# A fused attention and expert block: maxima 30 ahead of the scores, Q loads ahead of the shift, heads turned a step later

## The chip, the cores and the metric

The kernel runs on one core of a Trainium2 chip (eight cores; one is used). The metric is the device time of one execution in microseconds (us). Three executions of the kernel before took 608.63, 608.9 and 609.54 us; their median is 608.9.

## The reference

`x` has shape 8 x 512 x 128 (batch, token, channel). A modulation of 6 x 128 numbers per batch is computed from `c`. The block is attention and then a mixture of experts, each on a normalized and modulated input and each added back through a gate:

```python
mod = (_silu(L0_c) @ L0_wmod).reshape(L0_c.shape[0], 6, 1, -1)
h = _layernorm(x, axis=-1) * (1 + ca) + sa
x = x + ga * _L0_attn_ref(h, L0_attn_Wq, L0_attn_Wk, L0_attn_Wv)
h = _layernorm(x, axis=-1) * (1 + cb) + sb
x = x + gb * _L0_ffn_ref(h, ...)
# attention: 16 heads of 8 for the queries, one shared key and value head of 8
dist = jnp.einsum('bhqd,bkd->bhqk', q, k) * scale
dist = jax.nn.softmax(dist, axis=-1)
att = jnp.einsum('bhqk,bkd->bhqd', dist, v)
# experts: 8, of which the best 2 of each token, hidden size 512, gelu, weights by softmax of the two logits
```

## The kernel before, in words

The attention works on 8 batches of 16 heads. A group is 4 heads (`G`) of one batch, so there are 32 groups (`GROUPS`), four to a batch (`NG`). Each group has four steps `s` (128 keys each in the scores), and in each step a counter `j` runs from 0 to 3. Three products are made for a group:

- **maxima** (`maximum`, line 1052): 16 units of four matmuls each write a 128 x 512 block of scores into one of three banks of a ring; VectorE reduces it to a negative maximum per query (line 1364, `neg_max`).
- **scores** (`scores`, line 1068): K times Q, with the maximum already subtracted. For that the negative maxima must be in three extra rows of Q. The way there: VectorE transposes the group's maxima (`turn_maxima`, line 1372), GpSimd splits them into three bf16 parts (`split`, lines 76 to 79), and SyncE copies these with three DMAs into Q (`shift`, line 948). ScalarE takes the exponential (line 1252).
- **values** (`values`, line 1079): the exponentials times V, summed over the steps in one bank. ScalarE copies the bank out (line 1244), and SyncE spreads it over two tensors with five DMAs (`regroup`, lines 958 and 959).

Each engine has its own list of instructions in the order in which the code writes them, and waits by semaphores. DMAs are issued from SyncE's list in that order too. In the loop over `g`, `s` and `j` TensorE makes one unit of the maxima of group `g + 2` for each `j`, so the maxima run 32 units ahead of the scores; before the loop the first 32 units are made with little else beside them. VectorE's reductions follow in the same order. The scores of step 0 wait for the group's `shift_loaded`.

Q, K and V have two buffers, one batch in each. A **refill** loads the batch after next in six of the loop's groups (4, 8, ..., 24): SyncE waits until all values of the group before are done and issues ten DMAs, Q and K in turn, then V (`load_operands`, lines 148, 152 and 156). Their rows of Q are 24 partitions of 16 KB, and three such loads fill it.

When a batch's four groups are done, its sums and its heads are turned by TensorE (`turn_sums`, line 1089; `turn_heads`, line 1097) through the same ring of three banks, and copied out by ScalarE (`sums_out`, `heads_out`). This falls into the groups 5, 9, 13, ..., 29. From group 9 on these also hold the rank matmuls of an earlier batch (lines 1134 and 1135). `ring_order` lists all users of the ring in order; who frees a bank follows from it. A unit waits for the taking of the unit three places earlier.

GpSimd does the routing of earlier batches beside the splits (with indirect DMAs, line 812). The seventh batch is routed by VectorE in group 30. After the loop, 71 tiles of 128 tokens run through the experts (lines 1142, 1151 and 1162).

Of the kernel before, what the change touches and what calls it, by code (L numbers as in the profile page):

```python
# [13 lines left out]
B, S, D = 8, 512, 128  # L14
NH, DK = 16, 8
# [66 lines left out]
def adaln_block(nc, x, wq_t, wkv_t, router_t, w1_t, b1_t, w2_t, b2, c_t, wmod, constants, shift_rows, fill_rows, out):  # L82
# [8 lines left out]
    with ctx:  # L91
# [52 lines left out]
        def load_operands(eng, b, p, loaded, begin=0, end=3):  # L144

            for blk in range(begin, end):
# [3 lines left out]
                              ).then_inc(loaded[p], 16)  # L150
                for n in (0, 1):
# [3 lines left out]
            if begin == 0:  # L155
                eng.dma_start(V[p][:].rearrange("p t c -> p (t c)"), v_cols[b]).then_inc(loaded[p], 16)
# [472 lines left out]

        def ring_order():  # L630

            units = [("maximum", n // (G * T), n // G % T, n % G) for n in range(2 * G * T)]
            for g in range(GROUPS):
                for s in range(T):
                    for j in range(G):
                        if g + 2 < GROUPS:
                            units.append(("maximum", g + 2, s, j))
# [302 lines left out]
        with nc.Block() as block:  # L940
            @block.sync
            def _(eng):
# [65 lines left out]
                load_operands(eng, 1, 1, batch_loaded, 0, 3)  # L1008
# [34 lines left out]
            def _(eng):  # L1043
# [125 lines left out]
                for g in (0, 1):  # L1169
                    for n in range(G * T):  # L1170
                        b = g * (G * T) + n - 5
                        if b >= 0 and b % 3 == 0 and b // 3 < B:
                            modulation_row(b // 3)
                        maximum(g, n // G, n % G)
                eng.wait_ge(row_out, START + B)
                eng.wait_ge(rows_loaded, START + 7 * 16)
                for g in range(GROUPS):
                    for s in range(T):
                        for j in range(G):
                            if g + 2 < GROUPS:  # L1180
                                maximum(g + 2, s, j)
# [4 lines left out]
                            if s == 1 and j == 3 and batch_at(g, 1) is not None:  # L1186
# [52 lines left out]
            def _(eng):  # L1239
# [120 lines left out]
            def _(eng):  # L1360
# [119 lines left out]

                prepare_vector(eng)
# [5 lines left out]
                for n in range(2 * G * T):  # L1487
                    take_maximum(n // (G * T), n // G % T, n % G)
# [221 lines left out]
```

## Time and profile before

| what | us |
|---|---|
| median of three executions | 608.9 |
| the profiled execution's own time | 614.37 |
| its span, first to last instruction | 612.6 |
| TensorE matmul busy | 544.6 (89%) |
| VectorE busy | 503.6 (82%) |
| ScalarE busy | 435.9 (71%) |
| GpSimd busy | 306.5 (50%) |

The attention loop goes from about 66 to 422 us, the experts from there to the end. Rows of a timeline merge neighbours: "x16" is 16 instructions, the first number is the start of the first and the second the time from there to the end of the last. The bracket at the end is the engine's idle time before and who ended it.

### The profile page before, as it was taken

What the parts mean: (1) busy time and instruction counts of PE and PEld (TensorE: products, weight loads), DVE (VectorE), ACT (ScalarE), POOL (GpSimd) and SP (SyncE); (2) the same over time, 40 slices, a digit from 0 to 9 for tenths busy, and PEclk for the clock granted to TensorE, in tenths of its full rate; (3) what the DMA queues carried; (4) which work ended last, traced back from release to release, by engine and by line L of the source; (5) the groups of instructions that cost most, each with busy time, mean ns of one, the idle gap of its engine ahead of it and who ended that gap; (6) DMA issues with size and microseconds to landing.
All of it is one profiled execution on the core that took longest, in us unless ns stands there. A gap on an engine that the chain in (4) does not pass through costs nothing.

```text
span 612.6 us, 21006 instructions
## 1 busy us (share of the span) xinstructions
PE 544.6 (89%) x7675; PEld 337.3 (55%) x7675; DVE 503.6 (82%) x1190; ACT 435.9 (71%) x724; POOL 306.5 (50%) x581
## 2 busy tenths in 40 slices
PE   2669999999999999999999999968886896999970
PEld 2222345555555545545545545425876885999960
DVE  5878999999999899899899899876564673755697
ACT  5674588889888889889888888768443432566661
POOL 2615010134475676675775766760555465455470
PEclk9888999999999999999999999989997998899995
DMA  6289500220310410401401401111322122232645
GB/s 191 64 275 353 137 8 13 52 59 10 76 42 23 103 33 24 115 23 28 112 23 27 116 18 28 28 41 42 84 71 65 57 73 74 76 86 60 202 139 176
DMA packets 54484, 49.44 MB, mean 81 GB/s; under 512 B 20224, under 2 KB 48944, under 8 KB 53664
## 3 DMA queue, kind: packets, MB, share of 16 engines
q1 hardware_dynamic: 46864, 36.89, 22.4%
q0 software_dynamic: 4320, 9.38, 4.7%
q10 hardware_dynamic: 3200, 1.84, 1.0%
q8 instruction: 63, 1.03, 0.7%
q14 instruction: 37, 0.30, 0.2%
HBM read 29.40 MB, written 17.10 MB: 76 GB/s over the span
## 4 chain that ended last, share of the span: by engine, by line
PE 55%; DVE 15%; POOL 6%; issue 6%; another core or an unknown queue 5%; DMA 4%; SPq 3%; ACT 3%; DVEq 1%; POOLq 0%; ACTq 0%
PE ps L1052 13%; PE ps L1068 12%; PE ps L1079 12%; DVE neg_max L1364 7%; PE ps L1162 7%; PE ps L1151 7%; DMA Q<-max_parts 3%; POOL h_sorted L812 2%; ACT parts L1291 1%; PE ps L1142 1%; PE ps L1109 1%; DVE P L286 1%; SPq L948 1%; PE ps L1116 1%
## 5 line engine op out<-in xcount | busy, mean ns | idle before, releaser
L1364 DVE TENSOR_REDUCE neg_max<-ps 128x1 f32<-128x512 f32 x512 | 322.3, 681 | 19.3 <-PE ps L1052 15.9
L1252 ACT ACTIVATE P<-ps,zero 128x1024 f32<-128x1024 f32 x256 | 280.1, 1117 | 52.5 <-PE ps L1068 45.4
L1052 PE MATMUL ps<-K,Q 128*32 128x512 bf16 x2048 | 196.4, 382 | 4.3 <-DVE neg_max L1364 3.6
L1068 PE MATMUL ps<-Q,K 128*32 128x512 bf16 x2048 | 156.5, 381 | 5.7 <-ACT P L1252 3.6
L1079 PE MATMUL ps<-P,V 128*32 128x256 f32 x2048 | 157.8, 382 | 0.5 <-ACT P L1252 0.4
L1602 POOL DMA_INDIRECT y_rows<-P,to_now x71 | 72.2, 1017 | 87.5 <-DVE P L1427 46.0
L1291 ACT ACTIVATE parts<-ps,parts 128x128 f32<-128x128 f32 x228 | 63.8, 381 | 61.0 <-remote 23.7
L1052 PEld LDWEIGHTS ps<-K,Q 128*32 128x32 bf16 x2048 | 55.0, 96 | 74.7 <-DVE neg_max L1364 28.8
L1079 PEld LDWEIGHTS ps<-P,V 128*32 128x32 f32 x2048 | 61.9, 110 | 48.7 <-issue 3.0
L1068 PEld LDWEIGHTS ps<-Q,K 128*32 128x32 bf16 x2048 | 53.9, 97 | 61.1 <-ACT P L1252 11.6
L812 POOL DMA_INDIRECT h_sorted<-diag,slot x64 | 65.8, 1028 | 33.7 <-POOL max_parts L79 16.5
L1151 PE MATMUL ps<-parts 128*128 128x128 f32 x456 | 65.0, 284 | 7.4 <-issue 7.0
L1162 PE MATMUL ps<-W,parts 128*128 x456 | 63.0, 282 | 1.9 <-ACT parts L1291 0.9
L1151 PEld LDWEIGHTS ps<-parts 128*128 128x128 f32 x456 | 57.7, 196 | 10.6 <-issue 9.2
L1162 PEld LDWEIGHTS ps<-W,parts 128*128 128x128 f32 x456 | 57.2, 197 | 3.1 <-issue 2.7
L1408 DVE COPY parts<-W 128x644 f32 x57 | 30.4, 532 | 18.5 <-issue 10.7
L76 POOL CAST max_parts<-neg_max_T 128x32 bf16<-128x32 f32 x32 | 6.8, 213 | 72.6 <-DVE neg_max_T L1372 71.2
L1427 DVE TENSOR_TENSOR P<-ps,parts 128x128 f32<-128x128 f32 x57 | 16.2, 283 | 26.5 <-remote 16.3
L1291 ACT ACTIVATE P<-ps,P 128x128 f32<-128x128 f32 x56 | 16.0, 374 | 17.3 <-remote 8.2
L1142 PE MATMUL ps<-consts,xs 128*128 128x128 f32 x71 | 20.1, 283 | 1.2 <-DMA xs<-h_sorted 1.1
L1415 DVE COPY parts<-ps 128x128 f32<-128x128 f32 x57 | 16.2, 284 | 4.4 <-PE ps L1142 3.0
L1244 ACT COPY att_u<-ps 128x512 f32<-128x512 f32 x32 | 18.5, 579 | 0.8 <-PE ps L1079 0.8
(241 smaller groups left out, 542.9 us busy)
## 6 DMA issues: line engine op xcount, KB each, us to landing
Q<-q_parts SPq DMA_DIRECT2D x24, 384.0 KB
xs<-h_sorted SPq DMA_DIRECT2D x71, 72.0 KB
W<-w_t SPq DMA_DIRECT2D x2, 2048.0 KB, 11.0
q_parts<-parts SPq DMA_DIRECT2D x8, 384.0 KB, 3.7
Q<-y_rows SPq DMA_DIRECT2D x6, 512.0 KB
diag<-att_u SPq DMA_DIRECT2D x128, 16.0 KB
Q<-max_parts SPq DMA_DIRECT2D x96, 4.0 KB
out<-Q SPq DMA_DIRECT2D x6, 256.0 KB, 2.8
```

Of the source, the lines that this page charges most:

```text
L812: eng.indirect_dma_start(h_sorted, bass.IndirectOffsetOnAxis(ap=slot[p][:, k, t:t + 1], axis=0), hs[p][:, t, :], None).then_inc(routed[p], 16)
L1052: ins = eng.matmul(ring_bank(*unit)[QUAD * q:QUAD * (q + 1), :], Q[buffer_of(g)][:, g % NG * G + q, at:at + QUAD], K[buffer_of(g)][:, 0, : ...
L1068: ins = eng.matmul(to, K[p][:, 1, at:at + QUAD], Q[p][:, first:first + 2, some], start=True, stop=True, tile_position=(0, QUAD * q))
L1079: ins = eng.matmul(bank(7)[QUAD * j:QUAD * (j + 1), some], V[buffer_of(g)][:, s, :], P[s % 2][:, j, some], start=(s == 0 and u == 0), stop ...
L1142: eng.transpose(bank(TURN_BANK[t % 2])[:, 0:TS], xs[t % XD][:, 0:D], ident).then_inc(xsT_done, 1)
L1151: ins = eng.matmul(bank(t % UD)[:, TS * c:TS * (c + 1)], w1_now[t % HD][:, 128 * c:128 * (c + 1)], xsT[t % HD], start=True, stop=True)
L1162: ins = eng.matmul(bank(DOWN_BANK[t % 2])[:, 0:D], hid[t % HD][:, c, :], W2[:, bass.ds(e, 1), c, :].rearrange("p a d -> p (a d)"), start=( ...
L1252: nc.scalar.activation(P[s % 2][:, :, HALF * u:HALF * (u + 1)], bank(2 * u, 2).rearrange("p (j t) -> p j t", j=G), ACT.Exp, bias=zero[:], ...
L1291: nc.scalar.activation(hid[t % HD][:, c, :], bank(t % UD)[:, TS * c:TS * (c + 1)], ACT.Gelu, bias=w1_now[t % HD][:, F + c:F + c + 1]).then ...
L1364: eng.tensor_reduce(neg_max[g % 2][:, at:at + 1], ring_bank("maximum", g, s, j), AX.X, ALU.max, negate=True).then_inc(ring_used, 1)
L1408: eng.tensor_copy(w1_now[t % HD], W1[:, bass.ds(e, 1), :].rearrange("p a d -> p (a d)")).then_inc(w_copied, 1)
L1602: eng.indirect_dma_start(y_rows, bass.IndirectOffsetOnAxis(ap=to_now[t % YD], axis=0), ys[t % YD], None).then_inc(scattered[t % YD], 16)
```

## The change

It has three parts.

1. `LEAD` is 30 (2 x 16 - 2): 30 units of maxima are made ahead of the loop, and in the loop the unit of 30 places on. The transpose of a group's maxima comes at `j == 2` of step 0 where it came at `j == 0`. The routing of the seventh batch on VectorE moves from the head of group 30 behind its third unit.
2. `turn_heads` moves from `s == 1, j == 3` to `s == 2, j == 1`, and ScalarE's copy of it from the first to the second exponential of step 2.
3. The loads are split in two. `load_queries` (three DMAs) stands ahead of the shift in a refill group and waits for the scores of the group before; `load_others` (six of K, one of V) stays behind the regroup and waits for the values of the group before. The loads of the first two batches now also issue Q first and then K.

```diff
-        def load_operands(eng, b, p, loaded, begin=0, end=3):
+        def load_operands(eng, b, p, loaded):
+            load_queries(eng, b, p, loaded)
+            load_others(eng, b, p, loaded)
...
+        LEAD = 2 * G * T - 2
+        def place_of(n):
+            return n // (G * T), n // G % T, n % G
+        def ahead_of_scores(g, s, j):
+            return place_of((g * T + s) * G + j + LEAD)
...
                 for g in range(GROUPS):
                     b = g // NG + 1
+                    refill = g % NG == 0 and 2 <= b < B
+                    if refill:
+                        eng.wait_ge(score_done, START + g * T * 2)
+                        load_queries(eng, b, b % 2, batch_loaded)
                     if g + 1 < GROUPS:
                         shift(g + 1)
                     if 0 < g < GROUPS - 1:
                         regroup(g - 1)
-                    if g % NG == 0 and 2 <= b < B:
+                    if refill:
                         eng.wait_ge(pv_done, START + g * T * 2)
-                        load_operands(eng, b, b % 2, batch_loaded)
+                        load_others(eng, b, b % 2, batch_loaded)
...
-                            if g + 2 < GROUPS:
-                                maximum(g + 2, s, j)
+                            if ahead_of_scores(g, s, j)[0] < GROUPS:
+                                maximum(*ahead_of_scores(g, s, j))
...
-                            if s == 1 and j == 3 and batch_at(g, 1) is not None:
+                            if s == 2 and j == 1 and batch_at(g, 1) is not None:
                                 turn_heads(batch_at(g, 1))
...
-                            if s == 2 and u == 0 and batch_at(g, 1) is not None:
+                            if s == 2 and u == 1 and batch_at(g, 1) is not None:
                                 heads_out(batch_at(g, 1))
...
-                            if s == 0 and j == 0 and g + 2 < GROUPS:
+                            if s == 0 and j == 2 and g + 2 < GROUPS:
                                 turn_maxima(g + 1)
+                            if (g, s, j) == (GROUPS - 2, 0, 2):
+                                turn_maxima(g + 1)
+                                seventh_routed()
```

On SyncE, the DMAs of the first refill group. `Q<-max_parts` is the shift, `diag<-att_u` and `sums_T<-att_u` are the regroup, the others load the batch. Before, the rows are these:

```order
L948 DMA Q1<-max_parts1 1x64x32 [waits max_split]
L948 DMA Q1<-max_parts1 1x64x32 x2
L958 DMA diag<-att_u1 8x512 [waits att_out]
L958 DMA diag<-att_u1 8x512 x3
L959 DMA sums_T0<-att_u1 4x512
L148 DMA Q0<-q_parts 24x1x8192 [waits pv_done]
L152 DMA K0<-k_parts 24x4x128 x2
L148 DMA Q0<-q_parts 24x1x8192
L152 DMA K0<-k_parts 24x4x128 x2
L148 DMA Q0<-q_parts 24x1x8192
L152 DMA K0<-k_parts 24x4x128 x2
L156 DMA V0<-v_cols 128x128
```

And in the changed kernel, for the same group:

```order
L153 DMA Q0<-q_parts 24x1x8192 [waits score_done]
L153 DMA Q0<-q_parts 24x1x8192 x2
L965 DMA Q1<-max_parts1 1x64x32 [waits max_split]
L965 DMA Q1<-max_parts1 1x64x32 x2
L975 DMA diag<-att_u1 8x512 [waits att_out]
L975 DMA diag<-att_u1 8x512 x3
L976 DMA sums_T0<-att_u1 4x512
L162 DMA K0<-k_parts 24x4x128 [waits pv_done]
L162 DMA K0<-k_parts 24x4x128 x5
L165 DMA V0<-v_cols 128x128
```

The three loads of Q went from behind the shift and the regroup to ahead of them, and K is no longer issued between them.

On TensorE, group 13, from the third unit of step 1. The names: `ps<-K1,Q1` is a unit of the maxima, `ps<-Q1,K1` are scores, `ps<-P0,V1` values, `ps<-consts,diag` the turn of the heads, and `ps<-chosen1,counting` the ranks. Before:

```order
L1052 MATMUL ps<-K1,Q1 32x512 [waits ring_used]
L1052 MATMUL ps<-K1,Q1 32x512 x3
L1097 MATMUL ps<-consts,diag 128x128 [waits ring_copied]
L1097 MATMUL ps<-consts,diag 128x128 x3
L1134 MATMUL ps<-chosen1,counting 128x32 [waits ring_used,top_own]
L1135 MATMUL ps<-chosen1,counting 128x32
L1079 MATMUL ps<-P0,V1 32x256 [waits exp_done]
L1079 MATMUL ps<-P0,V1 32x256 x3
```

In the changed kernel:

```order
L1073 MATMUL ps<-K1,Q1 32x512 [waits ring_used]
L1073 MATMUL ps<-K1,Q1 32x512 x3
L1155 MATMUL ps<-chosen1,counting 128x32 [waits ring_copied,top_own]
L1156 MATMUL ps<-chosen1,counting 128x32
L1100 MATMUL ps<-P0,V1 32x256 [waits exp_done]
...
L1073 MATMUL ps<-K1,Q1 32x512 [waits ring_used]
L1073 MATMUL ps<-K1,Q1 32x512 x3
L1118 MATMUL ps<-consts,diag 128x128 [waits ring_copied]
L1118 MATMUL ps<-consts,diag 128x128 x3
L1100 MATMUL ps<-P1,V1 32x256 [waits exp_done]
```

The heads moved two units of the maxima on. What waited for the copy of the sums was the turn of the heads and is now the first rank matmul.

## Rows read from the trace of the kernel before

**Rows 1.** The page: busy time, clock in 40 slices, costliest group.
```profile
PE 544.6 (89%) x7675; PEld 337.3 (55%) x7675; DVE 503.6 (82%) x1190; ACT 435.9 (71%) x724; POOL 306.5 (50%) x581
PEclk9888999999999999999999999989997998899995
L1364 DVE TENSOR_REDUCE neg_max<-ps 128x1 f32<-128x512 f32 x512 | 322.3, 681 | 19.3 <-PE ps L1052 15.9
```

**Rows 2.** Waits, 88 to 109 us: total, times, longest.
```profile
ACT P L1252 <- PE ps L1068: 2.5, 13, 0.3
```

**Rows 3.** Timeline of VectorE: the transposes of maxima (start, us, ...).
```profile
109.31 0.20 DVE L1372 STREAM_TRANSPOSE neg_max_T<-neg_max 128x32 f32<-128x32 f32 x1
119.67 0.20 DVE L1372 STREAM_TRANSPOSE neg_max_T<-neg_max 128x32 f32<-128x32 f32 x1
...
152.97 0.20 DVE L1372 STREAM_TRANSPOSE neg_max_T<-neg_max 128x32 f32<-128x32 f32 x1
163.55 0.20 DVE L1372 STREAM_TRANSPOSE neg_max_T<-neg_max 128x32 f32<-128x32 f32 x1
...
330.13 0.20 DVE L1372 STREAM_TRANSPOSE neg_max_T<-neg_max 128x32 f32<-128x32 f32 x1
340.79 0.20 DVE L1372 STREAM_TRANSPOSE neg_max_T<-neg_max 128x32 f32<-128x32 f32 x1
```

**Rows 4.** The chain that ended last: start, us, what.
```profile
71.37 5.97 DMA Q<-max_parts
...
124.50 6.15 DMA Q<-max_parts
...
212.89 6.18 DMA Q<-max_parts
```

**Rows 5.** Line 1068 (scores): idle before it on TensorE, us and times.
```profile
  DMA Q<-max_parts: 2.2, 5
```

**Rows 6.** Timeline of SyncE's DMA issues.
```profile
111.17 1.81 SPq L948 DMA_DIRECT2D Q<-max_parts  x3
116.41 0.68 SPq L148 DMA_DIRECT2D Q<-q_parts  x1
117.13 1.89 SPq L152 DMA_DIRECT2D K<-k_parts  x2
123.28 1.82 SPq L948 DMA_DIRECT2D Q<-max_parts  x3
...
160.03 0.67 SPq L148 DMA_DIRECT2D Q<-q_parts  x1
...
204.22 0.67 SPq L148 DMA_DIRECT2D Q<-q_parts  x1
```

**Rows 7.** Timeline, ScalarE and TensorE at the start of groups 4 and 5.
```profile
107.90 1.11 ACT L1252 ACTIVATE P<-ps,zero 128x1024 f32<-128x1024 f32 x1 [0.18 <-PE ps L1068]
108.47 0.60 PE L1068 MATMUL ps<-Q,K 128*32 128x512 bf16 x8
...
118.83 0.60 PE L1068 MATMUL ps<-Q,K 128*32 128x512 bf16 x8
```

**Rows 8.** Windows: us, busy by engine, clock, DMA share, GB/s.
```profile
162.00:164.00 2.00, 2.00 (x44) 1.10 (x36) 2.00 (x5) 1.68 (x2) 1.52 (x6) 1.00 0.51 140
...
171.00:172.00 1.00, 1.00 (x28) 0.55 (x20) 1.00 (x3) 0.86 (x1) 0.73 (x4) 1.00 0.55 129
172.00:173.00 1.00, 1.00 (x24) 0.54 (x20) 1.00 (x3) 0.82 (x2) 0.82 (x3) 1.00 0.00 0
```

**Rows 9.** VectorE in group 13 (timeline), and waits of 263 to 274 us.
```profile
214.02 1.29 DVE L1364 TENSOR_REDUCE neg_max<-ps 128x1 f32<-128x512 f32 x2 [1.19 <-PE ps L1052]
215.22 0.54 DVE L1385 RECIPROCAL recip<-sums 128x64 f32<-128x64 f32 x1
...
PEld ps L1052 <- DVE neg_max L1364: 1.5, 5, 0.4
```

**Rows 10.** Timeline around the start of the loop.
```profile
58.05 9.91 DVE L1364 TENSOR_REDUCE neg_max<-ps 128x1 f32<-128x512 f32 x16
...
66.53 0.62 PE L1068 MATMUL ps<-Q,K 128*32 128x512 bf16 x8
```

**Rows 11.** Timeline of VectorE, the seventh batch's routing in group 30.
```profile
408.32 1.11 DVE L1398 TENSOR_SCALAR diag<-X,rstd,shift 128x128 f32<-128x128 f32 x4 [1.68 <-POOL shift L730]
```

More of the change, by code:

```diff
@@ L142, in adaln_block, with load_queries @@
         LOADS = 3 + 6 + 1
-        def load_operands(eng, b, p, loaded, begin=0, end=3):
-            for blk in range(begin, end):
+        def load_operands(eng, b, p, loaded):
+            load_queries(eng, b, p, loaded)
+            load_others(eng, b, p, loaded)
+        def load_queries(eng, b, p, loaded):
+            for blk in range(3):
                 rows = slice(QUAD * blk, QUAD * blk + 3 * DK)
@@ L150, in load_operands, with load_others @@
                               ).then_inc(loaded[p], 16)
+        def load_others(eng, b, p, loaded):
+            for blk in range(3):
+                rows = slice(QUAD * blk, QUAD * blk + 3 * DK)
                 for n in (0, 1):
@@ L628, in adaln_block @@
         TURN_LATE, LOGITS_LATE = (GROUPS - 1, 1, 1), (GROUPS - 1, 2, 3)
+        LEAD = 2 * G * T - 2
[3 more added lines that the diff above has]
+            return place_of((g * T + s) * G + j + LEAD)
         def ring_order():
-            units = [("maximum", n // (G * T), n // G % T, n % G) for n in range(2 * G * T)]
+            units = [("maximum", *place_of(n)) for n in range(LEAD)]
             for g in range(GROUPS):
@@ L635, in ring_order @@
                     for j in range(G):
-                        if g + 2 < GROUPS:
-                            units.append(("maximum", g + 2, s, j))
+                        if ahead_of_scores(g, s, j)[0] < GROUPS:
+                            units.append(("maximum", *ahead_of_scores(g, s, j)))
                         if s == 1 and j == 1 and batch_at(g, 1) is not None:
                             units.append(("sums turned", batch_at(g, 1)))
-                        if s == 1 and j == 3 and batch_at(g, 1) is not None:
+                        if s == 2 and j == 1 and batch_at(g, 1) is not None:
                             units.append(("heads turned", batch_at(g, 1)))
@@ L1007, in _ @@
                 eng.wait_ge(cleared, START + 8)
-                load_operands(eng, 1, 1, batch_loaded, 0, 3)
+                load_operands(eng, 1, 1, batch_loaded)
                 eng.wait_ge(row_out, START + B)
@@ L1168, in _ @@
                 eng.wait_ge(v_copied, START + B - 1)
[L1169 to L1174, printed above, removed]
+                for n in range(LEAD):
+                    b = n - 5
+                    if b >= 0 and b % 3 == 0 and b // 3 < B:
+                        modulation_row(b // 3)
+                    maximum(*place_of(n))
                 eng.wait_ge(row_out, START + B)
@@ L1185, in _ @@
                                 turn_sums(batch_at(g, 1))
-                            if s == 1 and j == 3 and batch_at(g, 1) is not None:
+                            if s == 2 and j == 1 and batch_at(g, 1) is not None:
                                 turn_heads(batch_at(g, 1))
@@ L1479, in late_add, with seventh_routed @@
                                       ALU.add).then_inc(tail_sum, 1)
+                def seventh_routed():
+                    eng.wait_ge(x1_own, START + (LAST - 1) * X1_OPS)
+                    eng.wait_ge(top_own, START + top_ops(LAST - 1))
+                    add_attention(eng, LAST - 1)
+                    for t in range(T):
+                        stats(LAST - 1, t)
+                    variance(eng, LAST - 1)
+                    full_tiles(eng)
+                    normalized(LAST - 1)
+                    rows(eng, LAST - 1)
+                    first_list(eng)
                 prepare_vector(eng)
@@ L1486, in _ @@
                 eng.wait_ge(pad_set, START + 2)
-                for n in range(2 * G * T):
-                    take_maximum(n // (G * T), n // G % T, n % G)
+                for n in range(LEAD):
+                    take_maximum(*place_of(n))
                     if n == G * T:
@@ L1491, in _ @@
                 for g in range(GROUPS):
-                    if g == GROUPS - 2:
-                        turn_maxima(g + 1)
-                        eng.wait_ge(x1_own, START + (LAST - 1) * X1_OPS)
-                        eng.wait_ge(top_own, START + top_ops(LAST - 1))
-                        add_attention(eng, LAST - 1)
-                        for t in range(T):
-                            stats(LAST - 1, t)
-                        variance(eng, LAST - 1)
-                        full_tiles(eng)
-                        normalized(LAST - 1)
-                        rows(eng, LAST - 1)
-                        first_list(eng)
                     if g == GROUPS - 1:
```

9 lines of the change are left out of this document (4 added, 5 removed).

## The prediction

> **What bounds the kernel now.** I read the page first: TensorE is busy for 89% of the span, VectorE for 82%, and TensorE's clock stands at its full level (2.4 GHz) in nearly all slices of the attention loop [rows 1]. The loop is where everything that the change touches lies. The waits of two quiet groups there name only ScalarE waiting for TensorE, 2.5 us in 13 pieces, and TensorE waits for nobody [rows 2]. So I took the length of a group from the transposes of the maxima, of which there is one per group: 109.31 to 119.67 is 10.36 us [rows 3]. VectorE's part of that is 16 reductions, 9.91 us where nothing holds them [rows 10], and the transpose of 0.20; so TensorE binds, with VectorE 0.2 us behind it. Groups are counted from 0 to 31, and group g starts with its first scores matmul (L1068); I write T(g) for that moment, T(4) = 108.47 and T(5) = 118.83 [rows 7]. A group is delayed where those scores must wait for their shift rows. The chain of waits shows this directly: "DMA Q<-max_parts" stands in it at 71.37, 124.50 and 212.89 and ends at 77.34, 130.65 and 219.07 [rows 4], just before groups 1, 6 and 14. All such idle time before scores is 2.2 us, in 5 waits [rows 5]. Groups 6 and 14 are the ones whose shift is queued on SyncE behind a refill. The first Q load of those refills is issued at 116.41 and 204.22 [rows 6].
>
> **Run ahead of 30.** The 32 maxima ahead of the first scores run at VectorE's pace, 16 in 9.91 us [rows 10]; with two fewer, the first scores (66.53) start about 1.3 us sooner. But VectorE's own order is not changed: the turn of group 1's maxima still follows the 33rd reduction, so its shift still lands at about 77.34 [rows 4], and the second group's scores wait for it 1.3 us longer than they did. From there on both programs stand at the same time, the new one with two maxima (about 0.2 us of array time each) still to do, which fall into group 30, where TensorE has room since it has no other maxima. Sum of this part: 0. Its ends are -1.4, if that shift came sooner, and +0.5, if the two maxima are paid in full. Every later group now has two units, 1.3 us, less between its last maximum and its shift's due time. Where SyncE is free and no load is ahead, that costs nothing: group 5's shift is issued at 111.17 [rows 6], 7.7 us ahead of its scores, and no scores of the quiet groups wait for theirs [rows 2]. In groups 2, 3 and 0 modulo 4 GpSimd is busy when the maxima are turned, which hides the later turn altogether. On VectorE the seventh batch's routing starts 1.3 us later in group 30; it has a wait of 1.68 us for GpSimd at its end [rows 11], which takes that up.
>
> **Q loads ahead of the shift.** There are six refills, at groups 4, 8, 12, 16, 20 and 24. Before, such a load stood on SyncE behind group g+1's shift and held up group g+2's. Now three Q loads of 384 KB stand ahead of group g+1's shift. They are released by the last scores of group g-1, as is the exponential at 107.90: 0.57 us ahead of T(4) [rows 7]. Three issues of 0.67 us occupy SyncE for 2 us [rows 6], which is hidden, because the split of the maxima ends later still. What counts is when the shift that is queued behind these loads lands. Before, from the first Q issue to the landing of the shift behind it, 124.50 + 6.15 - 116.41 = 14.2 us passed at group 4, and 212.89 + 6.18 - 204.22 = 14.9 us at group 12 [rows 4, 6]. In those times K and V loads of 208 KB went ahead of the shift too. A window inside such a load moves 140 GB/s with half of the DMA engines' time busy [rows 8], and at that rate 208 KB is 1.5 us, which leaves 12.7 us. The refill that starts at 160.03 has its queue dry at 172, 12.0 us later, with K, V and the shift's data all in it [rows 6, 8]. I take 12.1. Counted from T(g), the shift lands at -0.57 + 12.1 = 11.5 us. The scores that need it are due at 10.36 in group 4 and at 10.6 to 10.7 in the other five; of these the first (152.97 to 163.55) and the last (330.13 to 340.79) are shown [rows 3]. The new wait is 1.15 + 5 x 0.9 = 5.6 us. TensorE waits in its own queue, so the maxima behind these scores wait with it, and the lost time is lost to the loop. The low end: the Q data alone, 1.15 MB at 140 GB/s, is 8.2 us, and with about 1.4 us from issue to first bytes a landing at 9.1 after T(g), and no wait. The high end: nothing is saved against 14.2 us, a wait of 3 us in each, 18 us in all. I stay at 12.1 because the two refills that can be corrected for K and V, 12.0 and 12.7, lie next to it.
> The windows show that half of the DMA engines' time is in use while only Q data flow. The Trainium skill, page "DMA: Bandwidth & Descriptors", section "Why a DMA increments its semaphore by 16 and not by 1", says that a copy is split over the largest number up to 16 that divides the slowest dimension of both sides; with 24 and 8 that is 8 engines, each with nine rows of 16 KB to move. Its section "Queues, rings and completion order" says that each DMA engine takes one issuer's descriptors in ring order, and that the semaphore's write waits for every earlier write of that engine. By this rule the shift cannot land before the Q data has; without it, with the shift passing on idle DMA engines, the new waits would be 0 and the change would gain 2 us.
>
> **K and V later.** They follow the shift and the regroup now and are due two groups later. Before, they went out between 117.13 and 123.28 [rows 6], up to 14.8 us after T(4), and no maximum waited for them; now the last goes out about 13 us after T(g). Cost 0. Group g+2's shift now has only small transfers ahead of it: the waits of groups 6 and 14 go. By TensorE's pace of 0.22 us for four matmuls they are 0.3 and 0.4 us, with 0.1 elsewhere: 0.8 in all (bounds 0 and the 2.2 of [rows 5]).
>
> **Heads turned in the third step.** No instruction is added. The turn of the heads (four transposes in group 13's row of the order) stood with the two rank matmuls between two maxima, and VectorE idled 1.19 us there, then did a reciprocal of 0.54 [rows 9] and was late in the next group, where the weight loads for maxima waited 1.5 us for it in 5 pieces [rows 9]. Now the heads come where the reciprocal is, so the 0.54 runs inside the gap. Of the 1.5 us most is slack of the loader; 0.2 to 0.4 per refill period reaches the array. I take 1.3 us over the loop, bounds 0 and 6 x 0.54 = 3.2. ScalarE's copy of the heads moves by one exponential; the ring bank is asked for three units later, by which time the copy is made.
>
> **Sum.** 0 + 5.6 - 0.8 - 1.3 = +3.5 us. The profiled execution took 614.37 us (span 612.6), 5.5 above the median of 608.9; the difference carries over, 617.9 for such an execution and 608.9 + 3.5 = 612.4 for the median.
>
> **Rivals.** (1) The shift is not held by the Q data, or these finish by the time that the scores are due: waits at groups 5, 9, ... stay at 0 to 0.2 us, and what is left is the gain, -0.8 - 1.3 = -2.1: 606.8. For it: the low end above, and that half of the DMA engines' time stays free under a load. Against it: in both refills of the chain the shift landed more than 14 us after the first Q load, though it was issued only 6.9 us after it (116.41 to 123.28). It decides from a landing before 10.4 us after T(g). (2) The wait is at the high end, or it repeats in groups 6, 10, ... because the loop stays behind: +9: 618. For it: GpSimd's scatters add transfers from group 12 on (14.9 against 14.2). Against it: the K and V data no longer stand in front. (3) Nothing moves much: the earlier start at the front and the spared waits cancel the new ones: new waits of 0.3 each, -2.1 + 1.8: 608.6. This asks for a landing at about 10.9.
>
> **How the numbers follow.** Forecast (waits of about 1 us in six groups) 0.68, own range 610.2 to 615.2; rival 1 0.15; rival 2 0.08; rival 3 0.09. A difference under 0.2% (1.2 us) is what can't be told from no change. Faster 0.16, same 0.08, slower 0.76. The range of 8 in 10 goes from 607.5, which takes in rival 3, to 615.6.
>
> **What would show it.** In the profile after: the chain should hold "DMA Q<-max_parts" before groups 5, 9, 13, 17, 21 and 25, with gaps of about 1 us on TensorE, and no longer before 6 and 14; the transposes of the maxima after 4, 8, ... should lie 11.3 to 11.7 us apart. Group 1's scores should still start near 77.4, and after a longer wait. VectorE's idle of 1.19 us should shrink by half. If the shift in a refill group lands less than 10.4 us after T(g), the forecast is wrong in its main term; if the first groups start 1.3 us sooner and stay so, in its first.

## The result, and the profile after

The changed kernel takes 618.9 us (median of 4 executions, 617.2 to 624.2) against 609.2 of the kernel before: a ratio of 1.0185, 95% interval 1.0132 to 1.0238. It is slower, as forecast, but by 9.7 us and not by 3.5, and 618.9 lies outside the range of 607.5 to 615.6. The profiled execution took 617.22 us (span 615.4), the lowest of its four. That of before took 614.37, above all four timed executions (608.63 to 609.56). So their spans differ by 2.8 us only, and sums over the whole program are better taken from a pair of profiles that lie at their medians (b_before and b_after, below).

The page of after, answering to [rows 1]: the same busy times, the same clock in the loop. Nothing became more expensive; what grew is idle time, on VectorE 27.1 us before the maxima and not 19.3.
```profile
PE 544.7 (89%) x7675; PEld 339.2 (55%) x7675; DVE 504.6 (82%) x1190; ACT 435.7 (71%) x724; POOL 309.0 (50%) x581
PEclk9989999999999999999999999998998998799995
L1384 DVE TENSOR_REDUCE neg_max<-ps 128x1 f32<-128x512 f32 x512 | 322.5, 682 | 27.1 <-PE ps L1073 24.2
```

The chain of waits of after (start, us, what), answering to [rows 4]. The shift stands in it before groups 1, 5 and 9, no longer before 6 and 14, and not before 13, 17, 21 or 25:
```profile
69.50 5.63 DMA Q<-max_parts
...
111.67 5.75 DMA Q<-max_parts
...
155.62 5.80 DMA Q<-max_parts
```

TensorE's timeline at these scores, and under it the idle time of the matmuls of line 1089 by releaser (us, times):
```profile
75.17 0.61 PE L1089 MATMUL ps<-Q,K 128*32 128x512 bf16 x8 [1.04 <-DMA Q<-max_parts]
...
117.46 0.61 PE L1089 MATMUL ps<-Q,K 128*32 128x512 bf16 x8 [0.67 <-DMA Q<-max_parts]
...
161.47 0.61 PE L1089 MATMUL ps<-Q,K 128*32 128x512 bf16 x8 [0.26 <-DMA Q<-max_parts]
...
  DMA Q<-max_parts: 2.2, 4
```
The same sum over the matmuls alone in the kernel before is this:
```profile
  DMA Q<-max_parts: 0.4, 2
```
The 2.2 us in 5 waits of [rows 5] is not that number: it adds the idle time of the engine's weight loads (1.8 in 3) to that of the matmuls (0.17 at group 1 and 0.22 at group 14). So the array's waits for shifts grew from 0.4 to 2.2 us. The new waits in refill groups are 0.67 and 0.26 us of idle array, not 5.6 us. The rest of the 2.2 is the start: group 1 waits 1.04 for its shift, near the 1.3 that was forecast, and group 0 0.20.

The event that moved most is in group 30, which is itself hardly longer (14.67 us against 14.47). VectorE's timeline of after (start, us, engine, line, operation, in brackets the idle time before it and what ended it), and GpSimd's in the same stretch:
```profile
397.95 0.69 DVE L1384 TENSOR_REDUCE neg_max<-ps 128x1 f32<-128x512 f32 x1 [1.25 <-PE ps L1073]
400.15 0.69 DVE L1384 TENSOR_REDUCE neg_max<-ps 128x1 f32<-128x512 f32 x1 [1.51 <-PE ps L1073]
403.07 1.29 DVE L1384 TENSOR_REDUCE neg_max<-ps 128x1 f32<-128x512 f32 x2 [2.23 <-remote]
404.39 0.21 DVE L1392 STREAM_TRANSPOSE neg_max_T<-neg_max 128x32 f32<-128x32 f32 x1
...
414.43 1.12 DVE L1418 TENSOR_SCALAR diag<-X,rstd,shift 128x128 f32<-128x128 f32 x4
```
```profile
395.69 1.02 POOL L829 DMA_INDIRECT h_sorted<-diag,slot  x1 [0.54 <-POOL slot L822]
397.01 0.97 POOL L829 DMA_INDIRECT h_sorted<-diag,slot  x1 [0.30 <-issue]
...
400.84 0.97 POOL L829 DMA_INDIRECT h_sorted<-diag,slot  x1 [0.30 <-issue]
...
433.74 0.97 POOL L1626 DMA_INDIRECT y_rows<-P,to_now  x1 [17.86 <-DVE P L1447]
```
In before, the transpose of group 31's maxima stands at 396.78, VectorE's wait for GpSimd there is that of [rows 11], and the first scatter of the expert phase is at 428.94:
```profile
396.78 0.21 DVE L1372 STREAM_TRANSPOSE neg_max_T<-neg_max 128x32 f32<-128x32 f32 x1
...
428.94 0.97 POOL L1602 DMA_INDIRECT y_rows<-P,to_now  x1 [17.80 <-DVE P L1427]
```
So the transpose came 7.6 us later, the seventh batch's normalization 6.1 later (414.43 against 408.32), and the expert phase 4.8 later. Group 30's first scores stand at 395.49 in before and 397.72 in after, so 2.2 of these were there already. Two further reductions ahead of the transpose are 1.3 by the new order. The rest is VectorE's waiting for its last maxima (1.25, 1.51 and 2.23 us) while GpSimd made five scatters in a row (each about 1 us, 1.28 apart).

### The profile page after: what moved, and what is told of

Read it like the earlier page. It is cut to its first block, busy times and chain, and to the rows that moved or that the text cites. A ratio compares the mean times of both kernels' runs of the same rounds, so it can differ in the third digit from the quotient of the medians.

```text
span 615.4 us, 21006 instructions
## 1 busy us (share of the span) xinstructions
PE 544.7 (89%) x7675; PEld 339.2 (55%) x7675; DVE 504.6 (82%) x1190; ACT 435.7 (71%) x724; POOL 309.0 (50%) x581
## 4 chain that ended last, share of the span: by engine, by line
PE 61%; DVE 17%; DMA 6%; another core or an unknown queue 4%; issue 4%; SPq 2%; ACT 2%; POOL 1%; DVEq 1%; POOLq 0%; ACTq 0%
PE ps L1073 15%; PE ps L1100 14%; PE ps L1089 13%; DVE neg_max L1384 8%; PE ps L1172 8%; PE ps L1183 8%; DMA Q<-max_parts 3%; DMA k_parts<-parts 1%; DMA Q<-y_rows 1%; PE ps L1163 1%; PE ps L1130 1%; PE ps L1137 1%; DVE ln_stats L280 1%; DVE P L295 1%
## 5 line engine op out<-in xcount | busy, mean ns | idle before, releaser
L1384 DVE TENSOR_REDUCE neg_max<-ps 128x1 f32<-128x512 f32 x512 | 322.5, 682 | 27.1 <-PE ps L1073 24.2
L1626 POOL DMA_INDIRECT y_rows<-P,to_now x71 | 73.5, 1035 | 84.0 <-DVE P L1447 46.0
L1172 PEld LDWEIGHTS ps<-parts 128*128 128x128 f32 x456 | 57.3, 195 | 11.6 <-issue 10.2
L1311 ACT ACTIVATE P<-ps,P 128x128 f32<-128x128 f32 x56 | 16.0, 372 | 15.8 <-remote 6.9
```

The lines of the kernel that those rows point to most:

```text
L1172: ins = eng.matmul(bank(t % UD)[:, TS * c:TS * (c + 1)], w1_now[t % HD][:, 128 * c:128 * (c + 1)], xsT[t % HD], start=True, stop=True)
L1311: nc.scalar.activation(hid[t % HD][:, c, :], bank(t % UD)[:, TS * c:TS * (c + 1)], ACT.Gelu, bias=w1_now[t % HD][:, F + c:F + c + 1]).then ...
L1384: eng.tensor_reduce(neg_max[g % 2][:, at:at + 1], ring_bank("maximum", g, s, j), AX.X, ALU.max, negate=True).then_inc(ring_used, 1)
L1626: eng.indirect_dma_start(y_rows, bass.IndirectOffsetOnAxis(ap=to_now[t % YD], axis=0), ys[t % YD], None).then_inc(scattered[t % YD], 16)
```

## Experiments

A is the kind of chip of the first measurement, on which before takes 609 to 612 us and group 30 14.5; several chips of this kind were used. B is another chip, on which before takes 586 and group 30 9.9 (e4_first; before was not profiled there). Every ratio is against before on the same chip, and rows of different kinds of chip should not be subtracted. T(g) is as in the prediction.

| kernel | what differs | chip | ratio (95%) | us |
|---|---|---|---|---|
| e1_lead | before + run ahead 30, with its later transpose and routing | B | 1.0133 (1.0084 to 1.0182) | +7.8 |
| e2_heads | before + heads in step 3 | B | 1.0025 (1.0008 to 1.0042) | +1.5 |
| e2_again | the same | A | 1.0001 (0.9971 to 1.0031) | 0 |
| e3_qahead | before + refills' Q first | B | 1.0037 (1.0018 to 1.0056) | +2.2 |
| e4_first | before + Q, then K, V in every load | B | 1.0012 (0.9996 to 1.0028) | +0.7 |
| b_after | after | A | 1.0145 (1.0111 to 1.0179) | +8.8 |
| b_after_2 | after | A | 1.0128 (1.0082 to 1.0173) | +7.8 |
| e5_nolead | after, run ahead 32, transpose and routing back too | A | 1.0069 (1.0046 to 1.0091) | +4.2 |
| e6_noheads | after, heads back | A | 1.0106 (1.0080 to 1.0131) | +6.5 |
| t1_tail | after, run ahead 32 again from group 29 | A | 1.0172 (1.0128 to 1.0216) | +10.5 |
| t4_notail | the same, heads back | A | 1.0068 (1.0039 to 1.0097) | +4.2 |
| t2_actq | before, refills' Q from ScalarE | A | 1.0029 (0.9997 to 1.0060) | +1.8 |
| p_probe | before + 7 scatters | A | 1.0085 (1.0046 to 1.0123) | +5.2 |
| r_before | before, 4 scatters moved | A | 1.0029 (1.0002 to 1.0057) | +1.8 |
| r_after | after, the same | A | 1.0103 (1.0045 to 1.0162) | +6.3 |
| r_after_2 | the same | A | 1.0114 (1.0071 to 1.0156) | +7.0 |
| r_noheads | r_after, heads back | A | 1.0085 (1.0055 to 1.0115) | +5.2 |

The us are the ratio less one by before's median. The intervals are 1 to 3.6 us to either side, so a difference of two rows under about 2.5 us is not clear of the noise. None is faster than before.

**One part at a time.** The edits, shortened ("..." stands for arguments, and conditions that stay are left out):
```diff
-        LEAD = 2 * G * T          # the diff's LEAD alone: e1_lead
+        LEAD = 2 * G * T - 2
-  if s == 1 and j == 3: turn_heads # the heads' lines alone: e2_heads
+  if s == 2 and j == 1: turn_heads
+  load_queries(...) ahead of shift(g + 1), load_others(...) behind regroup(g - 1)   # e3_qahead
+  load_operands: three Q loads, then K and V                                      # e4_first
```


> The kernel before with the run ahead of 30 alone (with it, the seventh batch's routing on VectorE behind the last two maxima, inside group 30); heads and all loads as before. Prediction as on record: 0 (-1.4 to +0.5). Theory H (the move of the heads is what costs, because groups 13, 15, 17, 19 ... grew by 0.5 us each in the trace of after): +1 to +3, all of it behind group 29, from the turn of group 31's maxima that now waits for group 30 (404.4 against 396.8). Theory L (the run ahead is what costs, because every shift is due 1.3 us sooner): +5 or more, and the groups that follow a refill 1.3 us longer each than before, since the shift behind a refill lands 1.3 us later.

> The kernel before with the turn of the heads and ScalarE's copy of them in the third step alone. Prediction as on record: -1.3 (-3.2 to 0). Theory H: about +4 (0.5 us in each of the groups 13, 15, ..., 29, less 0.25 in 14, 18, 22, 26), seen as groups 13, 17, 21 of about 12.15 us. Theory L: 0, and the groups as long as before.

> The kernel before with the Q loads of the six refills ahead of the shift and K and V behind the regroup; the first two batches are loaded in the old order. Prediction as on record: 5.6 - 0.8 = +4.8 us, waits of about 1 us in groups 5, 9, 13, 17, 21, 25. Theories H and L both read the new waits of after (1.4 us in all) as all that this part costs: about +0.6, less if the run ahead of 32 gives each shift 1.3 us more time, which takes even the wait of 0.84 at group 5 away: then -0.8.

> The kernel before with one thing of the change that the prediction did not price: the first two batches, and the refills as a whole at their old place, load Q three times and then K and V, not Q, K, K in turn. If it explains why after stood 1.9 us ahead already when group 0's maxima were turned (56.05 against 57.93): -1.9 at that point and -1 to -2 at the end. If that lead was only the difference of two executions: 0.

The run ahead is the dearest part (+7.8, interval 4.9 to 10.7), which neither the prediction nor theory H had. Its profile shows what theory L expected: with the refill's loads at their old place, the shift behind them lands later against scores that come sooner. Idle time of the scores' matmuls by releaser, first of e4_first (the run ahead of 32, same chip), then of e1_lead, then of e3_qahead:
```profile
  DMA Q<-max_parts: 2.8, 4
```
```profile
  DMA Q<-max_parts: 8.7, 8
```
```profile
  DMA Q<-max_parts: 4.6, 7
```
Not all of these waits belong to refills: the scores of group 31 alone wait 1.47, 1.78 and 1.60 us in the three. Without them, and without 0.43 at group 0 of e1_lead, 1.3, 6.5 and 3.0 us are left. Group 5 took 13.11 us in e1_lead and 11.54 in e4_first, group 17 13.48 and 12.39. In e3_qahead the chain is the one that the prediction drew for its second part, six shifts, before groups 5, 9, 13, 17, 21 and 25 (first and last here):
```profile
111.92 5.99 DMA Q<-max_parts
...
331.76 7.86 DMA Q<-max_parts
```
So the Q step had the right chain where it was tried alone, and about half of the size: the six waits are 0.31, 0.52, 0.20, 0.56, 0.34 and 1.05, 3.0 us for 5.6 forecast. It pays part of that back, because groups 13, 17 and 25 then go without the old waits (11.59 each against 13.16, 12.39 and 12.02). The order of the first loads costs nothing that can be told.

**The whole, and less one part.**


> The kernel before, unchanged: a profile on the chip of these experiments, on which it takes 586.0 us and not 608.9. Every theory expects the groups of e4_first (the same order in the loop): 10.36 in quiet groups, waits for the shift after the refills of groups 4, 8, 12, 16 and 24 (11.5 to 13.2), and no stall of some microseconds in group 30, which the profile of before held on the other chip (14.47).

> The changed kernel, unchanged, on this chip. If the parts add up (7.8 for the run ahead, 1.5 heads, 2.2 refills' Q, 0.7 first loads, measured one at a time): +12. If the run ahead of 30 costs only through the shift that is queued behind a whole refill (theory S, read from e1_lead: groups 5, 9, 13, 17, 25 of 12.3 to 13.5), then with Q ahead of the shift that cost is not there, the landing follows the Q data as in e3_qahead, and the sum is 2.2 + 1.5 + 0.7 = +4.4 and what the late routing of the seventh batch costs. The measurement on the first chip (+9.7) lies nearer the first.

> The changed kernel with the run ahead back at 32 (and the seventh batch's routing back ahead of group 30). If the parts add up: 1.5 + 2.2 + 0.7 = +4.4, so 7.8 below after. By theory S: also +4.4, but after lies beside it, at most 2 above. If the growth of the heads' groups in after (12.15 in 13, 17, 21, 25, 29, and 11.7 in 15, 19, 23, 27) came from the heads, it is here too: then the groups are 12.15 and 11.7; if it came from the run ahead and the heads together, they are 11.8 and 11.08 as in e2_heads.

> The changed kernel with the turn of the heads back at its old place. If the parts add up: 7.8 + 2.2 + 0.7 = +10.7. By theory S: +2.9 and the late routing. Groups 13, 15, ..., 29 as in e3_qahead (11.59 and 11.08).

Neither reading of the sum came: b_after is +8.8, not +12 and not +4.4. This series ran on a chip of kind A, though it was expected on B. Without the run ahead 4.6 us of the 8.8 go (the intervals are 2.1 and 1.4 us to either side). Without the heads 2.4 go, which is not clear of the noise. The 1.9 that remain are a remainder and no measurement of the Q loads: with the heads alone at 0 (e2_again) and heads and Q loads together at 4.2 (e5_nolead), the same parts would give them 4.2. So whether the parts add up on A is not shown. Theory S fell: after is not within 2 us of e5_nolead. The pair of profiles at the medians says where 9.8 us of span lie. These are the first scores of groups 0 and 30 and the first expert scatter, of b_before and then of b_after:
```profile
65.05 0.40 PE L1068 MATMUL ps<-Q,K 128*32 128x512 bf16 x4
393.27 0.40 PE L1068 MATMUL ps<-Q,K 128*32 128x512 bf16 x4
...
426.32 0.97 POOL L1602 DMA_INDIRECT y_rows<-P,to_now  x1 [17.41 <-DVE P L1427]
```
```profile
66.12 0.40 PE L1089 MATMUL ps<-Q,K 128*32 128x512 bf16 x4
400.91 0.40 PE L1089 MATMUL ps<-Q,K 128*32 128x512 bf16 x4
...
436.68 0.97 POOL L1626 DMA_INDIRECT y_rows<-P,to_now  x1 [17.85 <-DVE P L1447]
```
Groups 0 to 29 take 334.8 and not 328.2 us (+6.6), from there to the first expert scatter 35.8 and not 33.0 (+2.7), the rest -0.6, and the start +1.1, which is no effect of the change: T(0) lay between 65.05 and 66.53 in the seven profiles on A with the run ahead of 32 (median 65.7), and between 63.84 and 66.12 in the nine with 30 (median 64.4).

Most of the loop's growth is there without the run ahead. In e5_nolead groups 0 to 29 take 333.6 us, 5.4 more than in b_before. The heads alone (e2_again) take 329.4, 1.2 more. In b_after the growth stands in groups 4, 8 and 12 (2.5 us), in group 0 (0.8), and in the groups that hold the turn of the heads or come two behind them, while groups 16, 20 and 24 are as long as before.

**What a scatter does to the others.** The idle times of group 30 suggested that signals between engines are late while GpSimd makes scatters. p_probe puts scatters where there were none (shortened):
```diff
+                    for n in {1: (0,), 2: (1, 2), 3: (3, 4, 5, 6)}.get(g, ()):
+                        eng.indirect_dma_start(probe_rows[n], ..., consts[:, 0:128], None)
```


> The kernel before with seven scatters more on GpSimd, of 128 rows of 512 bytes that nothing reads, in groups that had none: one in group 1, two in a row in group 2, four in a row in group 3. Theory G (while GpSimd makes a scatter's descriptors, the signals of the other engines arrive late, up to the scatter's end; read from group 30 of the profiles on the first two chips, where seven or eight scatters stand near each other and the group takes 14.4 to 16.9 us): group 1 10.4 to 10.8, group 2 10.5 to 11.5, group 3 12 to 14.5 instead of 10.36, and VectorE and ScalarE shown waiting for TensorE there; but on a chip like that of e1_lead to e4_first, where group 30 takes 10, all three stay at 10.36 to 10.6. Rival (group 30 is long because of its own work and not because of its scatters): all three 10.36 to 10.5 on either chip.

VectorE's timeline of p_probe in the group with four, and GpSimd's first and last scatter there:
```profile
87.38 0.20 DVE L1374 STREAM_TRANSPOSE neg_max_T<-neg_max 128x32 f32<-128x32 f32 x1
99.09 0.20 DVE L1374 STREAM_TRANSPOSE neg_max_T<-neg_max 128x32 f32<-128x32 f32 x1
...
104.06 0.69 DVE L1366 TENSOR_REDUCE neg_max<-ps 128x1 f32<-128x512 f32 x1 [1.21 <-PE ps L1054]
107.99 2.48 DVE L1366 TENSOR_REDUCE neg_max<-ps 128x1 f32<-128x512 f32 x4 [3.23 <-remote]
...
114.57 0.20 DVE L1374 STREAM_TRANSPOSE neg_max_T<-neg_max 128x32 f32<-128x32 f32 x1
```
```profile
101.72 1.01 POOL L1628 DMA_INDIRECT probe_rows<-consts,probe_at  x1 [0.79 <-POOL max_parts L79]
...
105.57 0.96 POOL L1628 DMA_INDIRECT probe_rows<-consts,probe_at  x1 [0.30 <-issue]
```
A quiet group is 10.36 us. With one scatter it stayed 10.36, with two in a row it took 11.4, with four 15.8 (more than the 12 to 14.5 expected), and the transposes lie 11.7 and 15.5 apart. The effect is that of the scatters: a group with one has room for it, one with four loses 5.4 us. Late signals are not all of it. TensorE's own eight matmuls of one `scores` product, which wait for a semaphore only ahead of the first, came in pieces in the same stretch and took 2.9 us where the product before took 0.60:
```profile
105.51 0.38 PE L1070 MATMUL ps<-Q,K 128*32 128x512 bf16 x1 [0.30 <-issue]
106.24 0.40 PE L1070 MATMUL ps<-Q,K 128*32 128x512 bf16 x2 [0.35 <-issue]
107.25 0.38 PE L1070 MATMUL ps<-Q,K 128*32 128x512 bf16 x1 [0.61 <-issue]
107.95 0.43 PE L1070 MATMUL ps<-Q,K 128*32 128x512 bf16 x4 [0.33 <-issue]
```
Whether the other engines' instructions, their signals or both are held up, these runs do not separate. On B the same five scatters stand around group 30 (e4_first), and VectorE has no gap at all there.

**The end of the loop.** If VectorE's last maxima are caught by the scatters, a return to the run ahead of 32 should free them.
```diff
+        CATCH_UP = [((GROUPS - 3) * T + T - 1) * G + 1, ((GROUPS - 3) * T + T - 1) * G + 3]   # two maxima in each
-                            if (g, s, j) == (GROUPS - 2, 0, 2):   # back ahead of group 30
-                                turn_maxima(g + 1); seventh_routed()
```


> The changed kernel, but the run ahead returns from 30 to 32 in the last step of group 29 (two slots with two maxima), so that group 31's maxima are turned and the seventh batch is routed ahead of group 30, as before the change. Theory T (the run ahead of 30 costs at the end, because VectorE's last two maxima, the turn and the routing stand behind group 30's late signals): 4 to 4.6 us below after on a chip with group 30 of 14 us or more, about 1 to 2 below on a chip where group 30 takes 10. Rival (prediction as on record: the two maxima fall into group 30 free): 0 to +0.5 against after.

> As t1_tail, and the turn of the heads back at its old place: what is left of the change is the run ahead of 30 up to group 29 and the Q loads first. Theories T and H together: before + 1.5 to + 2.5, the price of the Q loads alone. If the run ahead also costs inside the loop: before + 4 or more.

t4_notail did what theory T said. The turn of group 31's maxima moved from 6.6 to 2.0 us after T(30) and the first expert scatter from 37.7 to 33.6. The time fell from 1.0106 (e6_noheads) to 1.0068, with intervals that overlap, and +4.2 us is what was expected if the run ahead costs inside the loop too. t1_tail did not do it: its five scatters start 2.4 us ahead of T(30), in t4_notail 1.8 (in b_before 1.0), and the last maxima were caught all the same, with the turn 6.4 us after T(30). Over all 16 profiles on A, where the turn comes 6.4 us or more after T(30) (5 of them) the first expert scatter is 35.8 to 37.7 after it. In the seven with the turn at 2.0 or less and no scatter moved, it is 33.0 to 34.6. The medians of the two sets are 36.0 and 33.3, so a late turn goes with an end that is some 3 us longer. No edit has shown that as time saved clear of the noise.

**Moving the scatters instead.**
```diff
-                    if batch_at(g, 5) == CHUNK[0] - 1:
+                    if batch_at(g, 6) == CHUNK[0] - 1:
                         route(eng, CHUNK[0] - 1, 0)
                         route(eng, CHUNK[0] - 1, 1)
```


> The changed kernel, but four of the five scatters that GpSimd makes in a row around the start of group 30 come after its split of group 31's maxima (so they can't stand between TensorE's last maxima and VectorE). Theory B (the burst holds back the signals of the last maxima, and with them the turn of group 31's maxima and the seventh batch's routing): that turn comes 1.5 to 3 us after group 30's first scores and not 6.4, the first scatter of the expert phase 33 to 34 us after them and not 36, and the time is 2 to 4 us below after. Rival (order alone: VectorE's work of the seventh batch stands behind two more maxima, 1.3 us): the turn moves, the time stays within 1 us of after. On a chip where scatters hold nothing back: no change in either.

> The kernel before with the same four scatters moved. Theory B: the turn of group 31's maxima came in time there already (1.25 us after the first scores), so little is gained at that place: -1 to +1; the stalls move from group 30's start to its middle. If the burst as such costs wherever it stands, 0.

> As r_after with the turn of the heads at its old place. Theories B and H: 2.5 us below r_after, before + 2 to + 3, which is the price of the Q loads. If the run ahead of 30 costs in another way too: before + 5 or more, as e6_noheads (+6.5).

> The move of the heads alone, now on the chip of this call. If it is one on which a scatter holds back signals (group 30 of 14 us or more): +2 to +4, with groups 15, 19, 23, 27 of 11.6 us and not 11.15. If it is one on which it doesn't: +1.5 as measured.

> The changed kernel again, for comparison with the next on one chip. On a chip where group 30 takes 14 us or more: +8 to +10 against before, the turn of group 31's maxima 6.4 us after group 30's first scores.

> The changed kernel with the four scatters moved, again. Theory B: 2 to 4 us below b_after_2. Rival (the turn moves, but what it frees is lost to the same scatters later): within 1.5 us of b_after_2.

The turn moved as expected (2.0 after T(30)), but the first expert scatter still came 34.8 to 36.4 after T(30), and the time did not move: on one chip, r_after_2 and b_after_2 are the same within their intervals. The timeline of VectorE in r_after shows the new wait, twice that of [rows 11]: GpSimd makes six scatters ahead of the chain that normalizes the seventh batch.
```profile
413.04 1.11 DVE L1418 TENSOR_SCALAR diag<-X,rstd,shift 128x128 f32<-128x128 f32 x4 [3.63 <-POOL shift L747]
```
Theory B is therefore right on where the turn is held and wrong on what is gained by this edit. It cost before 1.8 us (interval 0.1 to 3.5). r_noheads, at +5.2, fits its second reading (+5 or more): the run ahead costs in another way too. e2_again fell short of the +2 to +4 expected: the heads alone cost 0 on A (interval -1.8 to +1.9), and groups 15, 19, 23 and 27 took 11.1 to 11.3 us, not 11.6.

**Does the queue hold the shift, or do the DMA engines?**
```diff
+ if u == 0 and s < 3 and refill: load_queries(nc.scalar, ..., blks=(s,))   # ahead of exponentials(g, s, 0)
```


> The kernel before with the refills' Q loads issued by ScalarE on its own DMA queue (one load ahead of the exponentials of each of the first three steps of the refill groups), K and V on SyncE behind the regroup, run ahead and heads as before; the first two batches load Q first. If the shift waits because it is queued behind the Q loads on SyncE's queue (the prediction's step), no scores wait for a shift in the refill groups or the next: 1.5 to 3 us below e3_qahead's place, so -1.5 to +0.5 against before. If it waits because the DMA engines themselves are busy with Q rows of 16 KB, whoever issued them: waits of 0.5 to 1.2 us stay, +1 to +3. Three issues on ScalarE may cost up to 0.5 us each where it has no slack.

Both. Of the waits for the shift one is left, before group 9, where a shift takes 6.99 us to land though no Q load stands ahead of it on its own queue (the chain, and the idle time before the scores):
```profile
155.16 6.99 DMA Q<-max_parts
```
```profile
  DMA Q<-max_parts: 0.8, 1
```
In its six refill groups the shift landed 8.8 to 11.5 us after T(g). With the Q loads on the same queue (e5_nolead, the same run ahead, also on A) it landed at 10.7 to 11.3, and with no load ahead (b_before) at 5.7 to 7.1. So leaving the queue spared 1.2 of 4.8 us on average, enough to meet most of the due times; the larger part of the delay stays while the Q rows flow from another queue. The comparison is not clean, since the three loads are here issued one by one, from 0.6 us ahead of T(g) to 4.2 behind it. What the waits gave back went elsewhere: groups 12, 16, 20 and 24 took 11.2 to 11.3 us and not 10.6, by waits between TensorE and VectorE.

## Why the prediction failed, step by step

The sum was 0 for the run ahead, -1.3 for the heads and +4.8 for the refills. In b_after it is +4.6, +2.4 and a remainder of +1.9. So the refills were priced too high, which hid a part of what the other two terms missed.

- **Run ahead, front.** Right in kind: by the medians on A the first scores come 1.25 us sooner (1.3 forecast), and T(1) - T(0) grew from 10.50 to 11.30 us (b_before, b_after). The sign "near 77.4" was no test, since T(1) of one and the same kernel was 75.2, 77.4 and 75.4.
- **Run ahead, end. This is the step that failed most.** "Two maxima ... fall into group 30, where TensorE has room", and the routing's 1.3 us is "taken up" by a wait of 1.68. TensorE has room there, but the trace of before showed group 30 at 14.47 us with five scatters in a row around its start, and I priced two units at the pace of a quiet group. They made the turn 4 us later than priced (6.4 to 6.7 us after T(30), not 2.6), more than the 1.68 that could hide. The term was 0 with an upper end of +0.5; measured (b_after less e5_nolead) it is +4.6, and alone on B +7.8. That the term was too small is shown; where all of it lies is not. Against e5_nolead 1.2 us are seen between T(30) and the first expert scatter and 1.2 in groups 0 to 29. Between e6_noheads and t4_notail 4.1 are seen in the first of these stretches. Taking the run ahead back from group 29 on (t1_tail) or moving the scatters (r_after_2) saved no time, so the turn's lateness is the place that is known, not the proven whole cause.
- **Q loads.** The mechanism was right, its size too large: 5.6 us of new waits were forecast, and they are 3.0 alone on B (e3_qahead), 0.9 in after (0.67 and 0.26) and 2.0 in b_after (0.58, 0.69 and 0.74, at groups 5, 9 and 13). In after, the shift lands 11.2, 11.0, 10.3, 9.9, 10.6 and 10.7 us after T(g), and 11.5 was forecast; from group 12 on that is in time. The Trainium skill, "DMA: Bandwidth & Descriptors", section "Queues, rings and completion order", has one issuer's descriptors served in ring order. The six shifts of e3_qahead and the one that is left in t2_actq, where ScalarE issues the Q loads, agree with it, but the landings of t2_actq (8.8 to 11.5 us after T(g), 5.7 to 7.1 with no load ahead) show that ring order is not all that held the shift.
- **Heads.** This step failed too: the gain of 1.3 us came nowhere. Alone they give 0 on A (interval -1.8 to +1.9) and +1.5 on B (0.5 to 2.5), and in after +2.4, not clear of the noise. The part that was read rightly is VectorE's idle time: the 1.19 of [rows 9] became 0.66, and the reciprocal now runs behind the unit at which the heads (212.46 on TensorE) hold up the maxima:
```profile
212.35 1.29 DVE L1384 TENSOR_REDUCE neg_max<-ps 128x1 f32<-128x512 f32 x2 [0.66 <-PE ps L1073]
213.55 0.54 DVE L1405 RECIPROCAL recip<-sums 128x64 f32<-128x64 f32 x1
...
217.13 3.08 DVE L1384 TENSOR_REDUCE neg_max<-ps 128x1 f32<-128x512 f32 x5 [0.56 <-PE ps L1073]
```
  But a new gap of 0.56 stands behind it, so the idle time of the group is not less: 0.39, 0.66 and 0.56 now, 0.15, 0.27 and 1.19 before. And two groups later another 0.5 us is lost where the Q loads go first as well. The transposes around group 23 in e5_nolead (heads late, Q first) lie 11.29 apart, in e2_again (heads late alone) 10.85:
```profile
320.91 0.20 DVE L1392 STREAM_TRANSPOSE neg_max_T<-neg_max 128x32 f32<-128x32 f32 x1
332.20 0.20 DVE L1392 STREAM_TRANSPOSE neg_max_T<-neg_max 128x32 f32<-128x32 f32 x1
```
```profile
317.94 0.20 DVE L1397 STREAM_TRANSPOSE neg_max_T<-neg_max 128x32 f32<-128x32 f32 x1
328.79 0.20 DVE L1397 STREAM_TRANSPOSE neg_max_T<-neg_max 128x32 f32<-128x32 f32 x1
```
  In e5_nolead ScalarE's gap of 0.87 ends just after a scatter does, which by its place in the group is 0.4 us earlier than in b_before:
```profile
321.08 1.09 POOL L829 DMA_INDIRECT h_sorted<-diag,slot  x1 [0.53 <-POOL shift L747]
322.43 1.11 ACT L1272 ACTIVATE P<-ps,zero 128x1024 f32<-128x1024 f32 x1 [0.87 <-PE ps L1089]
```
  That the scatter's place is the cause there is argued from this, not tried.
- **K and V later, and groups 6 and 14.** Right in kind: no maximum waits for them, and the chain no longer holds those shifts. What went is small: of the matmuls' 0.4 us of waits in before only the 0.22 at group 14 was such a wait.
- **Rivals.** Rival 2 named 618, nearly what came, but by waits for the shift in every refill group, which stayed small. The right number would have been for a wrong reason. Rivals 1 and 3 are out by the time. But by the waits alone rival 3 (0.3 us each, a landing at about 10.9) was nearer than the forecast: b_after has 2.0 us in six groups and a mean landing of 10.8.

Open: how the run ahead's 4.6 us divide between group 30 and what follows it (the profiles of the last 180 us differ by 6 us among themselves), how heads and Q loads together come to 5.4 us in groups 0 to 29, why the refills' waits in after are below those of e3_qahead, and what makes the two kinds of chip differ.

## What to carry to other kernels

Price a unit of work by the stretch in which it will stand, not by the quiet one: before calling a group "free", look at how long it takes and what its idle time is put down to. "Remote" or "issue" beside a row of indirect DMAs is a warning. Where three edits all move the same queues, ask for each pair what they do together: the run ahead of 30 adds 5.2 us of shift waits behind whole refills (e1_lead against e4_first, on B, 6.5 and 1.3) and 0.8 behind Q loads that go first (b_after against e5_nolead, on A, 2.0 and 1.2). And check over which instructions a sum of waits runs before it is set against another: [rows 5] counts weight loads, the sums shown here for the other kernels do not.

## What the hardware showed

- On some chips indirect DMAs of 128 rows on GpSimd (1.0 us each, 1.28 apart in a row) hold up the other engines: one in a group cost nothing, two in a row 1.05 us, four 5.4 (p_probe). VectorE waited up to 3.2 us for maxima whose matmuls were done, and TensorE's matmuls within one product came up to 0.6 us apart. On B nothing of it is seen in the loop.
- The program is 4% faster on B. Of the 25.2 us between the spans of b_before and e4_first, 22.2 lie behind the first expert scatter (181.5 against 159.3), where every tile of the experts has a scatter. That the scatters are the reason is not tried.
- A small transfer on its own queue is slowed by large ones from another: with 24 rows of 16 KB per load issued by ScalarE, the shift of SyncE took 6.1 to 8.9 us from first issue to landing in t2_actq, and 3.0 to 4.4 in b_before.
